# Router logits formed inside the two attention layers, and the routings' normalisation moved to ScalarE

## The reference

```
x = x + adaptive_conv(group_norm(x))
x = x + box_conv_3x3(group_norm(x))
t = tokens(x)                                   # 4096 tokens of 128 channels
t = t + softmax_attention(layer_norm(t))        # 8 heads of 16, within an image; a = att @ Wo + bo
t = t + moe_d(layer_norm(t))                    # 8 experts, hidden 256
t = t + linear_attention(layer_norm(t))         # elu features, within an image
t = t + moe_f(layer_norm(t))                    # 8 experts, hidden 512

def moe(x):                                     # x: normalised tokens
    logits = x @ router                         # 8 per token
    topk_vals, topk_idx = top_k(logits, 2)
    w = softmax(topk_vals)
    return sum over the two experts e: w_e * (silu(x @ gate_e) * (x @ up_e)) @ down_e
```

## Time and profile before

| | us |
|---|---|
| median of 3 runs | 880.28 (879.82 to 881.58) |
| the profiled execution | 884.63, its span 882.9 |

### The profile page before, as it was taken

One profiled execution on the slowest core, in us unless ns is written; L12 is line 12 of the kernel. 1 busy time (PEld: TensorE's weight loads), 2 busy tenths in 40 slices (PEclk: granted clock), 3 DMA queues, 4 the chain that ended last, 5 costly groups with the idle time before them and its releaser, 6 DMA issues. The chain is left out here.

```text
span 882.9 us, 17711 instructions
## 1 busy us (share of the span) xinstructions
PE 717.3 (81%) x5093; PEld 560.7 (64%) x5093; DVE 521.0 (59%) x1467; ACT 416.2 (47%) x1075; POOL 401.1 (45%) x436
## 2 busy tenths in 40 slices
PE   3996879899998762988999156568389999999996
PEld 1555656666665462757888145557268888888882
DVE  7447857777776358665555258885863333333334
ACT  2423436767675331565555255544244444444434
POOL 0003245556663033345664577700036676766740
PEclk9997969999998765699999688886569999999999
DMA  3001000000000051164333122205001111111118
GB/s 102 1 1 25 1 1 1 1 0 0 0 1 1 18 186 36 44 186 118 91 89 78 53 55 52 53 4 191 1 21 40 44 47 46 46 49 42 49 29 285
DMA packets 33974, 46.18 MB, mean 52 GB/s; under 512 B 8195, under 2 KB 22663, under 8 KB 33648
## 3 DMA queue, kind: packets, MB, share of 16 engines
q1 hardware_dynamic: 25040, 27.57, 9.8%
q0 software_dynamic: 8864, 17.72, 7.7%
HBM read 30.11 MB, written 15.60 MB: 52 GB/s over the span
## 5 line engine op out<-in xcount | busy, mean ns | idle before, releaser
L1986 DVE TENSOR_TENSOR f_h<-ps,f_silu 128x512 f32<-128x512 f32 x71 | 49.1, 692 | 121.5 <-ACT f_silu L1944 121.5
L1044 DVE TENSOR_REDUCE negmax<-ps 128x2 f32<-128x512 f32 x128 | 82.6, 687 | 44.3 <-PE ps L878 43.4
L1832 POOL DMA_INDIRECT f_xg<-f_normed,f_gather x71 | 68.9, 971 | 78.1 <-POOLq L1469 54.8
L1832 POOL DMA_INDIRECT d_xg<-d_normed,d_gather x71 | 67.6, 952 | 71.0 <-PE ps L1873 42.3
L1944 ACT ACTIVATE f_silu<-ps 128x512 f32<-128x512 f32 x71 | 42.4, 598 | 108.8 <-PE ps L1883 108.8
L1838 POOL DMA_INDIRECT f_results<-f_y,f_scatter x71 | 71.9, 1012 | 45.7 <-issue 32.0
L785 ACT ACTIVATE prob<-ps 128x512 f32<-128x512 f32 x128 | 69.6, 598 | 42.2 <-PE ps L897 42.1
L1262 POOL DMA_INDIRECT e_yg<-d_results,d_slot_u x64 | 61.5, 961 | 32.4 <-issue 18.6
L1904 PE MATMUL ps<-f_w_out,f_hT 128*128 x568 | 75.2, 276 | 0.6 <-DVE f_y L1992 0.6
L1904 PEld LDWEIGHTS ps<-f_w_out,f_hT 128*128 128x128 f32 x568 | 69.0, 192 | 0.9 <-issue 0.8
L1986 DVE TENSOR_TENSOR d_h<-ps,d_silu 128x256 f32<-128x256 f32 x71 | 30.0, 423 | 37.5 <-ACT d_silu L1944 36.7
(11 more groups left out here) (357 smaller groups left out, 1956.2 us busy)
## 6 DMA issues: line engine op xcount, KB each, us to landing
d_results<-d_y SPq DMA_DIRECT2D x71, 64.0 KB, 1.8
f_raw<-in_f_in SPq DMA_DIRECT2D x16, 256.0 KB, 3.0
f_ys<-f_results SPq DMA_DIRECT2D x8, 512.0 KB, 6.7
X<-in_x SPq DMA_DIRECT2D x4, 512.0 KB, 5.4
d_normed<-X SPq DMA_DIRECT2D x8, 256.0 KB, 2.0
d_raw<-in_d_in SPq DMA_DIRECT2D x8, 256.0 KB, 2.7
f_normed<-X SPq DMA_DIRECT2D x8, 256.0 KB, 2.0
f_w_out<-in_f_out SPq DMA_DIRECT2D x1, 2048.0 KB, 8.7
```

Of the source, the lines that this page charges most:

```text
L1044: nc.vector.tensor_reduce(negmax[:, :, h // HG, col:col + 1], ps[:, 2 + h % 2, :].rearrange("p (t k) -> p t k", t=2), AX_X, ALU.max, negat ...
L1832: nc.gpsimd.indirect_dma_start(xg[:, n % 4, :], None, moe.xn_dram, bass.IndirectOffsetOnAxis(ap=moe.gather[:, n:n + 1], axis=0)).then_inc( ...
L1986: nc.vector.tensor_tensor(h[:, n % 2, :], UP(n), silu[:, n % 2, :], ALU.mult).then_inc(h_ready, 1)
```

## The change

In words, part by part:

- The two routers are centred in adaptive_conv (the mean over the 128 input channels of each column is taken off), and for routing d the products Wo·router and bo·router are formed there: four more DMAs, one small matmul behind `convolve(1)`, two behind `convolve(3)` and three small DVE operations. With a centred router a raw token times the router, times 1/sigma, is the logit of the normalised token.
- In softmax_attention the value and the output weights get 8 columns more. ACT's `values` makes two more copies of 128x8 per image, scaled by sigma (logits_in), and `add_output` on DVE a second addition of 128x16. That gives d's logits, without 1/sigma and without the constant bo·router.
- In linear_attention SUM moves into OUT's bank of PSUM, and `sum_tokens` waits for `heads_ready` for it; the free bank takes transposed tokens (TT) and LOGITS. PE's loop is unrolled, ACT's repeats every 2 steps and no longer every 4. From step 12 on, two finished images a step are transposed by PE (2 transposes each), copied by ACT (tT, 128x256), multiplied by the router (2 matmuls of 8 columns each) and copied into the logits (128x16): `older_tokens`, called `late` at the end of a step. Images 0 to 13 are taken in steps 12 to 18, image 14 in step 19, image 15 in step 20, and its logits leave in step 21. In DVE's order `normalise` stands ahead of `combine_first` and `moments`.
- In the routings the transposes and the logits matmuls are gone. POOL forms mean and variance in eight 128x32 operations behind one iota; ACT takes the square root; DVE starts its first round of maxima right behind that iota (in d with one addition of the constant, 128x256, ahead of it) and takes the reciprocal and a shift (128x32 each) between the two rounds; ACT alone then normalises the 32 tiles into X for the stores. The gap between the two best logits is multiplied by 1/sigma. SP issues the weight loads ahead of the stores of X.

The core of the diff:

```diff
-def pipeline(eng, stages, items, width=4):
+def pipeline(eng, stages, items, width=4, unrolled=False, late=None, end_step=0):
...
+    rounds = 0 if unrolled else (end - start) // width
...
+    for s in range(start + width * rounds, max(items + max(lags), end_step)):
         step(Step(0, s, width), s)
+        if late is not None:
+            late(s)
...
+            def fold_routers():
+                nc.tensor.matmul(FOLD[:, 0:Moe.E], wo_T[:], top.routers[:, 0, :], start=True, stop=True)
+                nc.tensor.matmul(FOLD[:, Moe.E:], bo_wide[:], top.routers[:, 0, :], start=True,
+                                 stop=True).then_inc(fold_ps, 1)
...
-                                     V.rearrange("p (t h d) -> p t h d", t=2, d=HD), ACT.Copy).then_inc(v_ready, 1)
+                                     V[:, :, 0:C].rearrange("p t (h d) -> p t h d", d=HD), ACT.Copy)
+                for t in range(2):
+                    tile = bass.ds(2 * m + t, 1)
+                    last = nc.scalar.activation(top.logits_in[:, tile, :].rearrange("p t e -> p (t e)"), V[:, t, C:],
+                                                ACT.Copy, scale=top.ln_std[:, tile])
+                last.then_inc(v_ready, 1)
...
-                t = T[:, bass.ds(2 * n, 2), :].rearrange("p t c -> p (t c)")
-                nc.vector.tensor_tensor(t, OUT, t, ALU.add).then_inc(tok_ready, 1)
+                tiles = bass.ds(2 * n, 2)
+                nc.vector.tensor_tensor(T[:, tiles, :], OUT[:, :, 0:C], T[:, tiles, :], ALU.add)
+                nc.vector.tensor_tensor(top.logits[:, tiles, :], OUT[:, :, C:], top.logits_in[:, tiles, :],
+                                        ALU.add).then_inc(tok_ready, 1)
...
-        SUM = lambda b: ps[:, 4 * b + 2, 0:AW]
+        TT = lambda b: ps[:, 4 * b + 2, 0:PIX]
+        LOGITS = lambda b: ps[:, 4 * b + 2, PIX:PIX + 2 * Moe.E]
+        def finished(step):
+            first = 2 * (step - N + 4)
+            return [n for n in (first, first + 1) if 0 <= n < N - 2] + [n for n in (N - 2, N - 1) if step == n + 5]
         OUT = lambda b: ps[:, 4 * b + 3, 0:2 * AW].rearrange("p (t c) -> p t c", t=2)
+        SUM = lambda b: ps[:, 4 * b + 3, 2 * AW:3 * AW]
...
-            pipeline(act, [(-1, transposed), (0, parts), (-2, normed), (-3, rstds)], N, 4)
+            act.sem_inc(logit_ps, 2)
+            def tokens_transposed(at, first, last):
+                act.wait_ge(tT_ps, at.n + 1)
+                act.wait_ge(logit_ps, at.n + 1)
+                nc.scalar.activation(tT[:, at.b, :], TT(at.b), ACT.Copy).then_inc(tT_ready, 1)
+            def logits(at, first, last):
+                act.wait_ge(logit_ps, at.n + 3)
+                nc.scalar.activation(top.logits[:, bass.ds(2 * at.n, 2), :].rearrange("p t e -> p (t e)"),
+                                     LOGITS(at.b), ACT.Copy).then_inc(logit_ready, 1)
+            def older_tokens(s):
+                for n in finished(s - 1):
+                    logits(Step(0, n, 2), n == 0, n == N - 1)
+                for n in finished(s):
+                    tokens_transposed(Step(0, n, 2), n == 0, n == N - 1)
+            pipeline(act, [(-1, transposed), (0, parts), (-2, normed), (-3, rstds)], N, 2, late=older_tokens,
+                     end_step=N + 6)
...
             def sum_tokens(at, first, last):
                 pe.wait_ge(kf_ready, at.n + 2)
                 pe.wait_ge(sum_ready, at.n + 1)
+                pe.wait_ge(heads_ready, at.n + 1)
...
+            def transpose_tokens(at, first, last):
+                pe.wait_ge(tok_ready, at.n + 3)
+                pe.wait_ge(logit_ready, at.n + 1)
+                for t in range(2):
+                    ins = nc.tensor.transpose(TT(at.b)[:, t * P:(t + 1) * P],
+                                              T[:, bass.ds(2 * at.n + t, 1), :].rearrange("p t c -> p (t c)"), ident[:])
+                ins.then_inc(tT_ps, 1)
+            def token_logits(at, first, last):
+                pe.wait_ge(tT_ready, at.n + 3)
+                for t in range(2):
+                    ins = nc.tensor.matmul(LOGITS(at.b)[:, t * Moe.E:(t + 1) * Moe.E], tT[:, at.b, t * P:(t + 1) * P],
+                                           top.routers[:, 1, :], start=True, stop=True)
+                ins.then_inc(logit_ps, 1)
+            def older_tokens(s):
+                for n in finished(s - 1):
+                    token_logits(Step(0, n, 2), n == 0, n == N - 1)
+                for n in finished(s):
+                    transpose_tokens(Step(0, n, 2), n == 0, n == N - 1)
+            pipeline(pe, [(-1, transpose), (0, project), (2, output), (1, sum_tokens)], N, 2, True,
+                     late=older_tokens, end_step=N + 6)
...
-            pipeline(dve, [(-2, shifts), (0, features), (1, sums), (-3, combine_first), (-3, moments),
-                           (2, normalise), (3, add_tokens), (3, statistics)], N, 4)
+            pipeline(dve, [(-2, shifts), (0, features), (1, sums), (2, normalise), (-3, combine_first), (-3, moments),
+                           (3, add_tokens), (3, statistics)], N, 4)
...
-            sp.dma_start(router[:], router_dram).then_inc(router_in, 16)
+            sp.dma_start(moe.w_out[:], w_out_dram).then_inc(moe.weights_in, 16)
+            if split is not None:
+                for i in range(split.pieces):
+                    split.load(sp, i)
             groups = moe.xn_dram.rearrange("(p g t) c -> g p t c", p=P, t=GROUP)
             for g in range(TILES // GROUP):
...
+            nc.gpsimd.iota(descending[:], pattern=[[-1, E]], base=E, channel_multiplier=0,
+                           **whole).then_inc(descending_ready, 1)
+            stats = top.ln_stats
+            difference, spread = moment[:, 0, :], moment[:, 1, :]
+            nc.gpsimd.tensor_tensor(spread, stats[:, :, 2], stats[:, :, 5], ALU.add)
+            nc.gpsimd.tensor_tensor(top.ln_mean[:], stats[:, :, 1], stats[:, :, 4], ALU.add)
+            step(nc.gpsimd.tensor_tensor(difference, stats[:, :, 1], stats[:, :, 4], ALU.subtract))
+            nc.gpsimd.tensor_scalar(spread, spread, 1.0 / C, None, ALU.mult)
+            nc.gpsimd.tensor_scalar(difference, difference, 0.5, None, ALU.mult)
+            step(nc.gpsimd.tensor_scalar(top.ln_mean[:], top.ln_mean[:], 0.5, None, ALU.mult))
+            step(nc.gpsimd.tensor_tensor(difference, difference, difference, ALU.mult))
+            nc.gpsimd.tensor_tensor(top.ln_std[:], spread, difference, ALU.add).then_inc(var_ready, 1)
...
+            act.wait_ge(var_ready, 1)
+            nc.scalar.activation(top.ln_std[:], top.ln_std[:], ACT.Sqrt, bias=top.eps5[:]).then_inc(std_ready, 1)
+            act.wait_ge(shift_ready, 1)
+            for g in range(TILES // GROUP):
+                for t in range(g * GROUP, (g + 1) * GROUP):
+                    ins = nc.scalar.activation(xn[:, t, :], T[:, t, :], ACT.Identity, bias=ln_shift[:, t:t + 1],
+                                               scale=top.ln_rstd[:, t:t + 1])
+                ins.then_inc(xn_ready, 1)
...
-            norm_on_vector(dve)
-            with dve.Fori(0, 2) as i:
-                for t in range(TILES // 2):
-                    tile = i * (TILES // 2) + t
-                    ins = nc.vector.tensor_scalar(
-                        xn[:, bass.ds(tile, 1), :].rearrange("p t c -> p (t c)"),
-                        T[:, bass.ds(tile, 1), :].rearrange("p t c -> p (t c)"),
-                        top.ln_mean[:, bass.ds(tile, 1)], top.ln_rstd[:, bass.ds(tile, 1)], ALU.subtract, ALU.mult)
...
-            dve.wait_ge(logit_ready, TILES // GROUP + 2)
+            dve.wait_ge(descending_ready, 1)
             by_tile = lambda ap: ap.unsqueeze(2).broadcast_to([P, TILES, E])
             by_expert = lambda ap: ap.unsqueeze(1).broadcast_to([P, TILES, E])
+            if constant is not None:
+                step(nc.vector.tensor_tensor(logits[:], logits[:], by_expert(constant[:]), ALU.add))
...
                 if c == 0:
                     step(nc.vector.scalar_tensor_tensor(rest[:], chosen[:, 0], -1e30, logits[:], ALU.mult, ALU.add))
+                    dve.wait_ge(std_ready, 1)
+                    nc.vector.reciprocal(top.ln_rstd[:], top.ln_std[:]).then_inc(rstd_ready, 1)
+                    dve.wait_ge(rstd_ready, 1)
+                    nc.vector.scalar_tensor_tensor(ln_shift[:], top.ln_mean[:], -1.0, top.ln_rstd[:], ALU.mult,
+                                                   ALU.mult).then_inc(shift_ready, 1)
             nc.vector.tensor_tensor(both[:], chosen[:, 0], chosen[:, 1], ALU.add).then_inc(both_ready, 1)
-            nc.vector.tensor_tensor(rank[:], best[:, 1], best[:, 0], ALU.subtract).then_inc(gap_ready, 1)
+            step(nc.vector.tensor_tensor(rank[:], best[:, 1], best[:, 0], ALU.subtract))
+            nc.vector.tensor_tensor(rank[:], rank[:], top.ln_rstd[:], ALU.mult).then_inc(gap_ready, 1)
+            dve.wait_ge(consts_ready, 1)
```

(23 more changed lines are left out.)

151 lines of the change are left out of this document (82 added, 69 removed).

## The result

The changed kernel takes 866.16 us in the median of 4 runs (865.48 to 869.45), the kernel before 880.93; the ratio is 0.9835, 95% interval 0.9801 to 0.987. Its profiled execution has a span of 867.7 us, 15.2 less than before.

| block | before | after | change | forecast |
|---|---|---|---|---|
| the convolutions up to the loading of the attention's weights | 69.45 | 71.48 | +2.0 | +0.7 |
| from there to routing d | 233.28 | 233.43 | +0.2 | +1 |
| routing d | 62.31 | 43.55 | -18.8 | -18.8 |
| experts d | 126.32 | 126.26 | -0.1 | 0 |
| linear attention up to the last e_q but two | 89.79 | 99.86 | +10.1 | +9.7 |

A forecast was written before the change was run, and what follows sets the result against it. Bounds: DVE's chain behind a late first maximum in the routings, a ring of moments, ACT, e_q, combine in linear attention. Terms -37.8 + 9.7 + 12.5 + 1 + 0.7 = -13.9 took 880.28 to 866 us; range 860 to 872, with rivals 854 to 876.

The forecast's parts named there:

- the drain: End of linear attention, behind the last e_q but two: late logits of 14 images take 27.4 us against 14.94, +12.5 us.
- the softmax attention: Two more ACT copies and one DVE addition an image are absorbed: 0 to 4 us over 16 images, taken as +1.
- the convolutions: In adaptive_conv, three small matmuls with their waits cost +0.7 us, between 0.3 and 2.
- the ring: Linear attention's loop of moments, ACT, e_q, combine: `normalise` on it lengthens 11 steps by 0.88 us each, +9.7 us.
- The routings: Work ahead of DVE's first maximum goes: routing d gains 18.8 us, f 19.0, together -37.8.
- just in time: Routing f: ACT's Exp is done at 18.0 us behind the start, tile_hot, needed by the first columns, at 18.25.
- F: Rival, chance 0.05: in each routing DVE waits 3.4 us for POOL's statistics; 873 us.
- seven rounds of 3.9 us at 1.2 GHz: Linear attention's end: logits of 14 images, two a round, each round 3.9 us at the low PE clock; 27.4 us.
- B: Rival, chance 0.14: the ring doesn't bind or the drain runs at full clock; 850 with both, 857 with slow drain.
- C: Rival, chance 0.16: the drain is at 1.2 GHz throughout and its own work adds; 8 us more, 874 us.
- E: Rival, chance 0.09: ACT's 32 copies are late in routing f and partly d; 1.5 to 4 us more, 869.
- D: Rival, chance 0.07, slower: softmax attention's PE falls to 1.2 GHz in more images, 10 us each; 906 with four.

## Why the prediction was right, point by point

The median was forecast at 866 and is 866.16, and part of that closeness is luck. In the traces the change is -15.2 us against -13.9: the drain (3.0 less than forecast) and the softmax attention (0.9 less) were met by the convolutions (1.3 more), the experts (0.7), the ring (0.4) and the routings (0.2). The profiled execution then lay 3.3 above the median and not 4.35, which gave most of the 1.3 back.

- **The routings** (-37.8) measured -37.6. The first maxima moved as worked out. ACT's 0.388 a tile is what was taken between the two rows (0.40), and "just in time" held within 0.6 us, on either side: ACT was 0.6 early in the trace compared here and 0.35 behind tile_hot in seven others. The rival with late POOL statistics (F) did not come: in d the eight operations were done 3.13 us behind the block's start (308.04) where 2.7 was forecast, and DVE did not wait. The contention of DVE with POOL that the Trainium skill states ("SBUF — State Buffer", section "Who interferes with whom") was weighed with up to 1.6 us a routing against the change. In f's first round two operations took 0.52 and 0.51 in place of 0.42, 0.2 us in all. From the figures of the Trainium skill ("ScalarE: Activation LUTs", section "What ACT_TABLE_LOAD costs") an estimate for the 32 is 12.3 to 15.3 us, and the trace agrees with 12.41. The drain of 1.38 us that the Trainium skill adds to a load there does not show in this trace: Exp starts at 616.94, 0.02 us behind the load's end at 616.92.
- **The ring** (+9.7) measured +10.1, and two runs that change the order alone show 10.1 and 9.4. The mechanism held; the step's 6.1 was right, but as the sum of two effects: 5.75 is the step with `normalise` on the ring and ACT unrolled, and the gaps of ACT's loop shown above make up the rest. (The run with 5.75 had the late work elsewhere too; the gaps alone are isolated, by the two kernels that differ in ACT's loop only.)
- **The drain** (+12.5) was mis-sized: it measured +9.5. The step that failed is the one of seven rounds of 3.9 us at 1.2 GHz. The clock was 0.79 in the window, not near 0.5. At a clock of 1.00 a round of two images is 1.86 us (592.05 to 593.91) and not the 3.0 of all its pieces one behind the other: PE is busy 8.06 of 8.20 us there, so ACT's copies and the hand-overs lie beside PE's work. In the other direction, the prediction took half of 0.96 us for four matmuls of 8 columns; those eight records are four matmuls, so it is 0.96. Most of the cost lies at the end: 5.8 us behind DVE's last statistics, and 3.7 ahead of them. With +9.5 the drain stands about midway between the forecast's +12.5 and the +6.2 of a drain at full clock.
- **The convolutions** (+0.7) measured +2.0 in this trace; eleven others with the same code reach the weights' load at 69.75 to 71.17 us against 69.45 and 69.25 in the two of the old code. So it is 0.3 to 2.0, the bounds that were given; the value was low, and here too a small matmul was taken at half its 0.24 us.
- **The rivals.** B (no price on the ring) is refuted, C (all at 1.2 GHz) too. E (ACT late in f) did not come in the trace compared here and by at most 0.35 us in most others, far below its 1.5. D did not happen in the softmax attention, whose length changed by 0.2 us.

## What to carry to other kernels

An operation that lies in the shadow of another engine's answer is free, and moved to the other side of the wait it costs its whole length at every step: before reordering a pipeline's stages, see which engine idles at which point of the ring. Work that is added to a pipeline belongs into the idle time of its steps and not into its drain: here it filled PE until DVE was done, and behind that each round was a chain of hand-overs between PE and ACT that nothing hid. A change that gains much in one block can lose half of it in another: the table by blocks shows it, the total does not.

## What the runs showed that was not expected

- ACT in a loop answered DVE's moments in 0.48 us and unrolled in 0.28, Exp followed Ln by 0.41 against 0.33, and the jump back took 0.22 in every second step. On a ring of 5.75 us that was 0.4 us a step.
- Beside POOL's casts and subtractions a DVE operation with one input in SBUF (128x128, scale and offset by pointers) took 0.58 us on average in place of 0.26.
- With the same code, the blocks from the loading of the attention's weights to routing d took 7.4 us less in two traces than in the changed kernel's own, with a granted clock of 0.95 and 1.00 in its halves (104 to 200 and 200 to 296 us) and not 0.89 and 0.98.
